# Value products of two neighbouring double steps in one run, with six decay buffers, in an attention and expert layer on one core

## The reference

```python
q, kv   = layernorm(x), ctx
k_hop   = einsum('bhvc,vmhc->bhvm', qh, rpe[hops])   # a learnt vector for each pair of positions
C       = (qh @ kh.T / 8 + k_hop) * D                # D = exp(gate sums), causal
h       = (C / (max(|sum C|, exp(-max)) + eps)) @ vh
x       = x + headwise_layernorm(h) * (1 + ln_w) + ln_b
x       = x + base(layernorm(x)) + top-2 experts(layernorm(x))
```

## Time and profile before

| | |
|---|---|
| median of three runs | 3316.13 us (3313.09 to 3317.16) |
| the profiled execution | 3310.51 us, of which 3308.5 us are the span from the first to the last instruction |
| busy shares of the span | TensorE 89%, VectorE 73%, GpSimd 61%, ScalarE 59% |
| mean granted TensorE clock | 0.964 of 2.4 GHz |

### The profile page before, as it was taken

How to read it: one execution, slowest core, us unless ns; L and a number is a source line. 1 busy time by engine, 2 the same in 40 slices (tenths; PEclk the granted TensorE clock), 3 DMA queues, 4 the chain that set the end, 5 groups by cost and what they waited for, 6 DMA issues and landing times.

```text
span 3308.5 us, 69970 instructions
## 1 busy us (share of the span) xinstructions
PE 2938.0 (89%) x24660; PEld 1856.5 (56%) x24660; DVE 2417.6 (73%) x5103; ACT 1941.4 (59%) x4654; POOL 2023.2 (61%) x2195
## 2 busy tenths in 40 slices
PE   6777777777777777699999999999999999999998
PEld 4555454544544554366666666666666666666664
DVE  5655555555555555588888888888888888888875
ACT  3444444444444444477666676666766767667663
POOL 6777777777777777256455455564554645546554
PEclk8888899999999999799999999999999999999999
DMA  9999999999999999556556565565565655656542
GB/s 283 345 349 349 320 348 344 344 352 352 347 345 346 351 348 326 190 184 189 180 174 185 178 189 179 177 187 181 177 190 169 195 173 179 187 179 180 185 148 66
DMA packets 414909, 799.98 MB, mean 242 GB/s; under 512 B 107338, under 2 KB 213834, under 8 KB 412516
## 3 DMA queue, kind: packets, MB, share of 16 engines
q1 hardware_dynamic: 312516, 453.08, 43.6%
q0 software_dynamic: 82560, 270.60, 24.5%
q10 hardware_dynamic: 19488, 71.84, 5.6%
HBM read 618.02 MB, written 176.69 MB: 240 GB/s over the span
## 4 chain that ended last, share of the span: by engine, by line
PE 65%; DMA 16%; POOL 9%; issue 5%; DVE 4%; ACT 1%; SPq 0%; POOLq 0%; DVEq 0%; ACTq 0%
DMA arena<-in_L_xattn_rpe_dram,arena 15%; PE psum L1772 13%; PE psum L1689 9%; PE psum L1701 9%; PE psum L1724 9%; PE psum L1627 7%; PE psum L1600 6%; POOL arena L797 6%; PE psum L1616 4%; PE psum L1753 3%; PE psum L1776 3%; PE psum L1664 2%; POOL arena L782 2%; PE psum L1569 1%; DVE arena L1237 1%
## 5 line engine op out<-in xcount | busy, mean ns | idle before, releaser
L797 POOL DMA_INDIRECT arena<-in_L_xattn_rpe_dram,arena x768 | 731.8, 953 | 235.0 <-issue 181.6
L1600 PE MATMUL psum<-arena 128*128 128x128 f32 x4128 | 614.4, 297 | 190.3 <-DMA arena<-in_L_xattn_rpe_dram,arena 178.6
L1600 PEld LDWEIGHTS psum<-arena 128*128 128x128 f32 x4128 | 488.9, 151 | 422.9 <-DMA arena<-in_L_xattn_rpe_dram,arena 292.9
L993 ACT ACTIVATE arena<-arena 128x512 f32<-128x512 f32 (+3 forms) x1024 | 496.3, 555 | 43.7 <-PE psum L1724 39.2
L1772 PE MATMUL psum<-arena 128*128 128x512 f32 x1024 | 493.3, 595 | 0.0
L1347 DVE TENSOR_TENSOR arena<-psum,arena 128x1024 f32<-128x1024 f32 (+1 forms) x384 | 386.6, 1041 | 133.3 <-PE psum L1701 122.4
L573 DVE COPY arena<-psum 128x512 f32<-128x512 f32 x384 | 263.4, 689 | 239.3 <-PE psum L1600 235.5
L582 DVE COPY arena<-psum 128x416 f32<-128x416 f32 (+15 forms) x512 | 225.3, 442 | 278.4 <-PE psum L1616 270.1
L823 POOL TENSOR_SCALAR_AFFINE_SELECT arena<-arena 128x256 f32<-128x256 f32 x256 | 118.7, 464 | 503.9 <-ACT arena L993 491.6
L1616 PE MATMUL psum<-arena 64*32 64x416 f32 (+7 forms) x8192 | 361.5, 422 | 59.3 <-ACT arena L909 38.1
L573 ACT COPY arena<-psum 128x512 f32<-128x512 f32 x384 | 225.8, 588 | 251.7 <-PE psum L1600 248.7
(11 more groups left out here) (112 smaller groups left out, 4632.1 us busy)
## 6 DMA issues: line engine op xcount, KB each, us to landing
arena<-in_x_dram SPq DMA_DIRECT2D x256, 256.0 KB, 4.1
arena<-gate_rows SPq DMA_DIRECT2D x128, 512.0 KB, 4.4
arena<-in_x_dram SPq DMA_DIRECT2D x512, 64.0 KB
arena<-in_ctx_dram SPq DMA_DIRECT2D x32, 1024.0 KB, 7.5
out_dram<-arena SPq DMA_DIRECT2D x128, 256.0 KB, 2.9
arena<-in_L_xattn_rpe_dram,arena POOLq DMA_INDIRECT x1032, 7.1
arena<-hop_products SPq DMA_DIRECT2D x128, 128.0 KB, 2.6
arena<-hop_products SPq DMA_DIRECT2D x128, 120.0 KB, 2.5
```

The source lines that it names most:

```text
L797: nc.gpsimd.indirect_dma_start(out=rows[set_of(n, v)][:, t, :], out_offset=None, in_=rpe[:, :], in_offset=bass.IndirectOffsetOnAxis(ap=her ...
L993: last = nc.scalar.activation(decay[u % DECAYS][:, e, at:at + width], top_pair[p % 2][:, e * S + j * P:e * S + j * P + width], ACT.Exp, bi ...
L1600: last = nc.tensor.transpose(turn_bank(o)[:, q * P:(q + 1) * P], own[:, q * P:(q + 1) * P], ident)
```

## The change

The value products of units 0 to 3 stand at the end of double step 1, those of units 4 and 5 stay at the end of step 2, units 6 to 9 stand at the end of step 4, units 10 and 11 stay at the end of step 5. Steps 0 and 3 have none. The order of the semaphore counts follows, and there are six decay buffers instead of four, so that ScalarE's exponentials of unit `u` wait for the value product of unit `u - 6`.

```diff
-    DECAYS = 4
+    DECAYS = 6
     DOUBLES = UNITS // 2
+    WEIGHED = {1: (0, 1, 2, 3), 2: (4, 5), 4: (6, 7, 8, 9), 5: (10, 11)}
...
         for d in range(DOUBLES):
-            pe_a_steps += [("score", 2 * d), ("score", 2 * d + 1), ("value", 2 * d), ("value", 2 * d + 1)]
+            pe_a_steps += [("score", 2 * d), ("score", 2 * d + 1)] + [("value", u) for u in WEIGHED.get(d, ())]
...
                     if ra:
-                        weigh(2 * d)
-                        weigh(2 * d + 1)
+                        for u in WEIGHED.get(d, ()):
+                            weigh(u)
```

## The result

The kernel is slower by 0.4%: 3326.41 us, the median of seven runs (3325.1 to 3332.38), against 3315.44 for seven runs of the kernel before (3312.81 to 3317.27). The ratio is 1.0037 [1.0027, 1.0047]. The forecast was 3307.8 us and its range ended at 3319. The profiled execution took 3325.42 us, with a span of 3323.4.

What follows compares the result with a forecast made beforehand. TensorE was taken as the bound almost without a gap, 59.85 of 59.88 us a round; -9.6 + 2.1 - 0.8 = -8.3 us, so 3316.1 - 8.3 = 3307.8 us, range 3299 to 3319.

Steps and rivals of the forecast that it cites:

- The merges: Value products of two double steps run together, twice a round: each saves 0.15 us of overhead, 9.6 us less in all.
- The direct change: Steps 0 and 3, array going from 128*128 straight to 64*128: scores behind it keep their 0.21 us overhead, 1.50 us.
- rival 2: Direct change to 64*128 saves less than said: 3317.4 us if as dear as two, 3311.6 if only a tail goes; chance 0.13.
- The copy of the keys: ScalarE's copy of context tile 3, step 1: ScalarE free 0.07 us late, 30 times, 2.1 us more.
- Rival 3: ScalarE's copy of context tile 3 late, TensorE waits: 0.52 us makes it over 0.2% slower, at worst 3362 us; chance 0.11.
- The last round: Last attention round: unit 3's value product waits 0.83 us for its mul, now covered by two products: 0.8 us less.
- The gate rows: Start of step 5, hardly any cover for `gate_stats`: no loss taken, since 0.20 us come free at L1443; bounds 0 and 0.15.
- rival 1: The wait at the gate rows takes the second merge back: costs 4.8 us, giving 3312.6 us; chance 0.20.
- Step 2: Scores 2 and 3 come 1.87 us earlier, costed at nothing; mul 4 waits for its hop scores as before.

## Why the prediction was wrong

**The merges: right.** The run of four takes 3.16 us, which was the forecast: 0.15 us over its 3,584 columns, where two pieces had 0.15 each. The direct change costs as it was taken (1.49 us for the scores, forecast 1.50), so rival 2 didn't hold.

**The copy of the keys: right in place and size.** From their start to the value products the transposes of step 1 took 1.943 us before and 2.028 after, as the median of the steady rounds: 0.085 us late, forecast 0.07. With the copies moved ahead they take 1.944. Rival 3's large lateness didn't come. (Its 0.52 us for a kernel slower by 0.2% leaves out the 0.8 us of the last round; with it, it is 0.55.)

**The last round: right.** After, the value products of step 1 start there without idle time (3232.19).

**The gate rows: right for this kernel.** VectorE's L1444 in step 3 takes 0.68 us, not the 0.87 of the earlier trace rows, with the residual tile in earlier. ScalarE's L1077 ends 0.30 us before the gate rows start at 2060.82, so rival 1 didn't hold (VectorE and ScalarE, after):

```profile
2048.68 0.68 DVE L1444 TENSOR_TENSOR arena<-arena 128x512 f32<-128x512 f32 x1
```

```profile
2059.89 0.63 ACT L1077 ACTIVATE arena<-arena 8x512 f32<-8x512 f32 x1 [3.76 <-DVE arena L1338]
```

Without the first merge the gate rows are late in the rounds where the residual tile is late, with the second merge or without it. I had the mechanism of those loads, but didn't see that what the second merge saves shows only where they come in time.

**Step 2: the step that failed.** Of scores 2 and 3 going ahead by 1.87 us I followed mul 2 and 3 as far as VectorE's idle time, and the loads, and wrote "I cost this at nothing"; of GpSimd I wrote only that "GpSimd's masks of units 4 and 5 follow earlier exponentials; mul 4 waits for its hop scores as before". Both halves are true, and together they make the loss. Mul 2 and 3 came earlier, and with them VectorE's value mean 0 and GpSimd's row of instructions behind it; mul 4 stayed. So GpSimd's row, which hangs on mean 0, slid by some 1.7 us against VectorE's work behind mul 4, which hangs on TensorE. I had followed the moved work to the next wait on each engine, not to what it then runs beside. And I had looked for a lack of cover at the gate rows alone: the gate product of step 2, whose wait for the sum of pair 0 stood in no list of mine, had none, as its 0.15 us behind the sum show. The sum had no term for that: 28 x 0.89 = 25 us more.

The balance of a round: -0.30 for the merges, +0.09 for the copy, +0.87 for the gate product (its start behind the value products of units 4 and 5) and -0.06 at the transposes and the router's product of step 2, which six buffers alone bring too, give +0.60; measured +0.59. The forecast had nothing for this last term, so it is partly luck that with the wait taken out the round is 59.62, where 59.6 was forecast; the kernel then takes 3303.97 us, where 3307.8 was.

The signs of it stood in the trace of before: the scaling took 0.57, 0.38 and 0.44 us for means 1 to 3, where it takes 0.17 for mean 0. All forms of a line by their durations (minimum, median, maximum in ns), before and after:

```profile
L1302 DVE TENSOR_SCALAR arena<-arena x128: 173/380/828, 1344.8 to 3173.5; 128x8 f32<-128x8 f32 x128
```

```profile
L1303 DVE TENSOR_SCALAR arena<-arena x128: 172/174/1248, 1344.4 to 3188.7; 128x8 f32<-128x8 f32 x128
```

The median of the line fell to 174 ns while its longest grew to 1,248. The line's sum grew by 15 us (49.5 to 64.4), and VectorE's busy time still fell by 11. The median and the engine's busy time hide what happened; the instruction that stood ahead of the sum of the pair decided.

## What to carry to other kernels

When work moves on one engine, list what moves with it on the others, and what stays; then look at which instructions now run side by side, not only at who waits for whom. Where one piece of work waits for another and starts the same short time behind its end in every round, take it that there is no cover, even if no wait is listed. A small instruction whose durations spread widely in the profile may be held by a neighbour: compare its ends with the neighbour's, and if they fall together, put it into idle time or on the neighbour's engine. A load's place in a queue can hide a saving on the bounding engine, so test each half of a change alone before dropping either.

## What the runs showed beyond that

A scaling of 128x8 elements on VectorE can take 1.23 us, seven times its 0.17, when it starts beside an instruction of GpSimd, and its end then follows GpSimd's by 0.03 us, whether it started 0.07 or 0.73 us into it; sums over 128x512 elements beside the same instructions keep their 0.68 us. A saving of 0.15 us came in each of the two places where the value products of two double steps run together.
